# Router of 16 batches, fewer waits and another order on VectorE in a fused cross-attention and routed FFN

## The chip, the cores and the metric

The kernel runs on one core of one Trainium2 chip. The metric is the device time of one execution in microseconds (us), the median of several runs.

## The reference

`x` and the context are 128 batches of 128 tokens by 256 features, in float32. There is one layer, with 16 heads of 16 features:

```python
x = x + xattn(layernorm(x), ctx)      # q from x, k and v from ctx; softmax(q k / 4) v, then @ Wo + bo
n = layernorm(x)
scores = n @ w_router                 # per batch, 128 scores
top = top_k(scores, 96)               # of 128 tokens, in each batch
ffn = n, with rows `top` replaced by gelu(n[top] @ w_block)
x = x + ffn
```

The kernel finds the 32 tokens that are dropped, not the 96 that are kept: four rounds of "find the 8 largest of the negated scores, replace them".

## The kernel before

One batch is one tile of 128 x 256. All engines run the same software pipeline over s = 2 .. 127, each with its own order of calls written out by hand; semaphores alone tie them together. `upto(b)` is the count that a semaphore has once batch b is done. In pass s:

- TensorE: `scores(s)`, `transpose_inputs(s+5)` (normalised x and context), `values(s-1)`, queries or keys of a pair of batches (one of the two in each pass), `keep_columns`, `candidates` (each once in a group), `projection(s-2)`, `block_product(s-4)`, `transpose_x1(s-3)`, `attention(s-1)`. q, k and v are made in three matmuls of split float32 (hi and lo parts).
- ScalarE: `attention_copy(s-2)`, `gelu_tanh(s-7)`, `inputs_high(s+5)` (hi part of the transposed inputs), and 16 exponentials with their sums, in four blocks j = 3, 2, 1, 0 of four. `exp_ready[j]` signals each block.
- VectorE: `x1_transposed`, statistics, four `maxima(s, j)`, `inputs_low(s+5)` (lo part), `values_and_bias(s-1)` (makes v_sb), reciprocals, the biases of q or k, `residual(s-2)` (makes x1), `final(s-16)`, `stats2`, `product_scaled(s-4)` (makes z), and the router's steps.
- GpSimd: `normalise(s+7)`, reciprocal square roots, `values_over_sums(s-1)` (makes v_pad for attention), the polynomial and the products of gelu, x + bias, `unprocessed(s-16)` (the part of the result that the FFN leaves unprocessed).
- SyncE issues the loads of two batches at a time, eight copies that lay out each pair's queries (q_eo), and the stores of pairs.

PSUM has five banks for scores (bank J serves j = 0 in odd batches; the router's transposes share it), one for transposed inputs and z, one for attention, v and projection, one for q, k and transposed x1.

The router works on GROUP = 8 batches: `candidates(b)` transposes the scores of 8 batches to 8 partitions, `router(b, 0)` negates them, steps 1 to 8 are four times a maximum (MAX8) and a replacement (MATCH_REPLACE8), step 9 makes the row of kept tokens, `keep_columns(b)` transposes it back, step 10 makes `half_keep` and `drop_rstd`, and `scale_and_shift(b)` on GpSimd makes alpha and beta. `unprocessed` and `final` of the group follow. x1 and z are kept in rings of R = 16 batches. After pass 127 the end is written out by hand: it runs the last group's router once z(127) is there, then `unprocessed` of 8 batches (3 on GpSimd, 5 on ScalarE) and 8 finals on VectorE.

A wait is `engine.wait_ge(semaphore, count)`. In the program an instruction takes one of the waits in front of it along; the others become instructions of the sequencer.

Of the kernel before, what the change touches and what calls it, by code (L numbers as in the profile page):

```python
# [6 lines left out]
def cross_attention_routed_ffn(  # L7
# [33 lines left out]
    GROUP = 8  # L41
# [6 lines left out]
    with ctx:  # L48
# [41 lines left out]
        mv2 = sb("mv2", [P, R, 2])  # L90
        ve2 = sb("ve2", [P, R])
        rstd2 = sb("rstd2", [P, R])
# [104 lines left out]
        U_ON_ACT = tuple(range(B - 13, B - 8)) + tuple(range(B - 5, B))  # L197
# [6 lines left out]
        def _(sp):  # L204
# [16 lines left out]
            def store(b):  # L221

                if b % 2 == 0 and has(b):
                    sp.wait_ge(final_ready, upto(b + 1))
                    sp.dma_start(out[b:b + 2, :, :].rearrange("b t e -> t b e"),
                                 z_sb[:, b % R:b % R + 2, 0:E]).then_inc(stored[pair(b)], 16)
# [41 lines left out]
            for s in range(0, B + 18):  # L268
                queries_even_odd(s + 3)
                load_c(s + 8)  # L270
                store(s - 17)
# [5 lines left out]
        def _(pe):  # L277
# [24 lines left out]

            def scores(b):
# [4 lines left out]
                if h == 0:  # L308
                    pe.wait_ge(q_eo_in[r2], (b // 4 + 1) * 128)
                    pe.wait_ge(k_ready, upto(b + 1))  # L310
                if has(b - 1):
                    pe.wait_ge(exp_ready[3], upto(b - 1))
                    pe.wait_ge(exp_ready[1], upto(b - 1))
                    pe.wait_ge(exp_ready[2], upto(b - 1))
                if has(b - 2):
                    pe.wait_ge(exp_ready[0], upto(b - 2))
                if b % GROUP == 5 and has(b - 13):
                    pe.wait_ge(cand_ready, upto(b - 13 + 7))
                if b % GROUP == 1 and has(b - 17):
                    pe.wait_ge(keep_col_ready, upto(b - 17 + 7))  # L320
# [8 lines left out]
            def transpose_inputs(b):  # L329
# [3 lines left out]
                pe.wait_ge(xhat_ready, upto(b))  # L333
                if b % 2 == 0:
                    pe.wait_ge(c_in[pair(b)], landed(b))
# [14 lines left out]
            def transpose_x1(b):  # L350
# [3 lines left out]
                pe.wait_ge(x1_ready, upto(b))  # L354
# [6 lines left out]
                for c in range(C):  # L361
                    mm = nc.tensor.transpose(ps_xt[:, c * T:(c + 1) * T], x1_sb[:, b % R, c * P:(c + 1) * P], ident[:, :])
                mm.then_inc(xt_mm, 1)

            def attention(b):
# [3 lines left out]
                pe.wait_ge(v_pad_ready, upto(b))  # L369
# [29 lines left out]
            def block_product(b):  # L399
# [3 lines left out]
                pe.wait_ge(xt_ready, upto(b))  # L403
# [7 lines left out]
            def queries_or_keys(b, kind):  # L411
# [3 lines left out]
                w = "qk"[kind]  # L415
                if kind == 0:
                    pe.wait_ge(t_lo_ready, upto(b + 1))
# [4 lines left out]
                else:  # L422
                    pe.wait_ge(t_lo_ready, upto(b + 1))
# [12 lines left out]
            def projection(b):  # L436
# [3 lines left out]
                pe.wait_ge(o_ready, upto(b))  # L440
# [7 lines left out]
            def candidates(b):  # L448

                if b % GROUP == 0 and has(b):  # L450
                    pe.wait_ge(z_ready, upto(b + 7))
                    pe.wait_ge(exp_ready[0], upto(b + 11))
                    r = b % R
                    nc.tensor.transpose(ps_cand, z_sb[:, r:r + GROUP, E], ident[:, :]).then_inc(score_mm, 8)

            def keep_columns(b):

                if b % GROUP == 0 and has(b):
                    pe.wait_ge(keep_row_ready, upto(b + 7))
                    pe.wait_ge(exp_ready[0], upto(b + 15))  # L460
                    nc.tensor.transpose(ps_keep, keep_row[:, :], ident[0:GROUP, 0:GROUP]).then_inc(keep_mm, 8)
# [16 lines left out]
            queries_or_keys(4, 0)  # L478
            attention(0)

            for s in range(2, B - 1):
                scores(s)
                transpose_inputs(s + 5)
# [650 lines left out]
```

## Time and profile before

| | |
|---|---|
| median of 3 runs | 938.55 us (938.32 to 939.42) |
| the profiled execution | 938.16 us |
| its span, first to last instruction | 936.2 us |
| TensorE matmul, weight load busy | 896.5, 758.3 us |
| VectorE, ScalarE, GpSimd busy | 880.6, 875.5, 798.4 us |
| granted TensorE clock, mean | 0.988 |
| scores(12), scores(127) start at | 105.60, 901.92 us |

In the rows PE is TensorE's matmuls, PEld its weight loads, DVE VectorE, ACT ScalarE, POOL GpSimd, SPq SyncE's queue of DMA issues. L324 is line 324 of the kernel. A row of the timeline has start, duration, engine, line, operation, what it writes and reads, the number of merged instructions, and in brackets the engine's idle time before it and what ended it. The profile names x1_sb and x_sb alike as x_sb.

### The profile page before, as it was taken

To read this page: it belongs to the slowest core of one execution; us is meant where nothing else is said; L and a number is where in the kernel's file an instruction comes from. 1 tells how busy PE (TensorE), PEld (TensorE's weight loads), DVE (VectorE), ACT (ScalarE), POOL (GpSimd) and SP (SyncE) were. 2 spreads that over 40 slices of the span, in tenths; PEclk is the share of its full clock that TensorE was granted. 3 is DMA by queue.
4 is the path that set the end of the run, shared out by engine and by line. 5 is a ranking of instruction groups with operands and counts; after the bars stand their busy time and mean duration, and the time that the engine had idled before them with its cause. 6 is when DMAs were issued, how large, how long until landed. Compare 5 with 4: busy or idle time off the path is not lost. (4 is left out here: it accounts for less than half of the span.)

```text
span 936.2 us, 32893 instructions
## 1 busy us (share of the span) xinstructions
PE 896.5 (96%) x10296; PEld 758.3 (81%) x10296; DVE 880.6 (94%) x2318; ACT 875.5 (94%) x4499; POOL 798.4 (85%) x1488
## 2 busy tenths in 40 slices
PE   6899999999999999999999999999999999999972
PEld 5688888888888888888888888888888888888861
DVE  4898999999999999999999999999999999999877
ACT  2899999999999999999999999999999999999983
POOL 4367789999999999999999989999999999998865
PEclk8999999999999999999999999999999999999997
DMA  6222222232232232232223123223223223211102
GB/s 186 74 52 59 64 69 56 82 92 55 85 91 59 83 89 72 72 87 73 73 85 92 55 85 92 57 82 92 59 83 91 58 85 88 79 54 54 47 25 91
DMA packets 71244, 70.84 MB, mean 76 GB/s; under 512 B 12192, under 2 KB 62880, under 8 KB 71072
## 3 DMA queue, kind: packets, MB, share of 16 engines
q1 hardware_dynamic: 71072, 68.73, 25.6%
q8 instruction: 85, 1.39, 0.7%
q14 instruction: 87, 0.71, 0.2%
HBM read 35.13 MB, written 16.78 MB: 55 GB/s over the span
## 5 line engine op out<-in xcount | busy, mean ns | idle before, releaser
L532 ACT ACTIVATE e_sb<-ps_s,neg_max 128x128 f32<-128x128 f32 x2048 | 717.2, 411 | 8.3 <-DVE neg_max L644 8.2
L532 ACT ACTIVATION_READ_ACCUMULATOR e_sb<-ps_s,neg_max 128x1 f32 x2048 | 515.4, 252 | 0.0
L644 DVE TENSOR_REDUCE neg_max<-ps_s 128x4 f32<-128x512 f32 x512 | 330.5, 667 | 35.7 <-PE ps_s L324 35.2
L324 PE MATMUL ps_s<-q_eo,k_sb 32*128 32x256 f32 x2048 | 147.6, 401 | 9.7 <-DMA q_eo<-q_raw 3.6
L377 PE MATMUL ps_a<-e_sb,v_pad 128*32 128x128 f32 x4096 | 138.4, 276 | 2.1 <-POOL v_pad L969 0.7
L294 PE MATMUL ps_a<-w_o_sb,o_sb 128*128 128x256 f32 x512 | 135.7, 387 | 2.3 <-DVE v_sb L736 2.0
L969 POOL TENSOR_TENSOR v_pad<-v_sb,recip 128x256 f32<-128x256 f32 x128 | 79.4, 620 | 67.8 <-DVE recip L688 62.5
L294 PE MATMUL ps_t<-w_z_sb,xt_sb 128*128 128x258 f32 x512 | 132.7, 381 | 1.4 <-DVE z_sb L747 1.4
L324 PEld LDWEIGHTS ps_s<-q_eo,k_sb 32*128 32x128 f32 x2048 | 95.6, 185 | 39.0 <-issue 33.4
L377 PEld LDWEIGHTS ps_a<-e_sb,v_pad 128*32 128x32 f32 x4096 | 104.1, 109 | 24.0 <-issue 21.7
L959 POOL TENSOR_TENSOR x_sb<-x_sb,bo_sb 128x256 f32<-128x256 f32 x128 | 119.0, 931 | 0.2
L294 PEld LDWEIGHTS ps_t<-w_z_sb,xt_sb 128*128 128x128 f32 x512 | 97.3, 191 | 15.5 <-issue 2.0
L543 ACT CAST t_hi<-ps_t 128x512 fp32r<-128x512 f32 x127 | 74.5, 587 | 30.7 <-PE ps_t L347 28.4
L294 PEld LDWEIGHTS ps_a<-w_o_sb,o_sb 128*128 128x128 f32 x512 | 87.2, 189 | 13.8 <-issue 4.9
L1015 POOL TENSOR_TENSOR g_sb<-g_sb,z_sb 128x256 f32<-128x256 f32 x128 | 90.2, 705 | 0.3
L695 DVE TENSOR_TENSOR t_lo<-ps_t,t_hi 128x512 fp32r<-128x512 f32 x127 | 86.5, 681 | 0.9 <-ACT t_hi L543 0.8
L287 PE MATMUL ps_a<-w_v_hi,t_hi 128*128 128x256 f32 x256 | 83.4, 326 | 1.3 <-ACT o_sb L551 1.2
L1029 POOL TENSOR_TENSOR z_sb<-g_sb,z_sb 128x256 f32<-128x256 f32 x121 | 82.4, 681 | 0.0
L287 PE MATMUL ps_q<-t_hi,w_q_hi 128*128 128x256 f32 x256 | 73.0, 285 | 3.8 <-DVE t_lo L695 2.2
L998 POOL TENSOR_TENSOR g_sb<-z_sb 128x256 f32<-128x256 f32 x123 | 75.3, 612 | 0.3 <-DVE z_sb L747 0.3
L287 PE MATMUL ps_q<-t_hi,w_k_hi 128*128 128x256 f32 x256 | 72.7, 284 | 0.2 <-issue 0.2
L287 PE MATMUL ps_q<-t_hi,w_q_lo 128*128 128x256 f32 x256 | 72.7, 284 | 0.0
(92 smaller groups left out, 2199.2 us busy)
## 6 DMA issues: line engine op xcount, KB each, us to landing
x_sb<-in_x SPq DMA_DIRECT2D x64, 256.0 KB, 2.9
c_sb<-in_ctx SPq DMA_DIRECT2D x64, 256.0 KB, 3.1
q_eo<-q_raw SPq DMA_DIRECT2D x512, 32.0 KB, 2.0
out<-z_sb SPq DMA_DIRECT2D x64, 256.0 KB, 2.4
z_sb<-in_L_xattn_Wkv SPq DMA_DIRECT2D x2, 256.0 KB, 5.2
z_sb<-in_L_xattn_Wq SPq DMA_DIRECT2D x1, 256.0 KB, 3.1
w_z_sb<-in_L_ffn_w_block SPq DMA_DIRECT2D x1, 256.0 KB, 5.7
w_o_sb<-in_L_xattn_Wo SPq DMA_DIRECT2D x1, 256.0 KB, 3.0
```

Source lines behind the costliest of these rows:

```text
L287: last = nc.tensor.matmul(dst, lhs(a, c), rhs(b, c), start=(c == 0 and n == 0), stop=(c == C - 1 and n == len(terms) - 1))
L294: last = nc.tensor.matmul(dst, lhs(c), rhs(c), start=(c == 0), stop=(c == C - 1))
L324: mm = nc.tensor.matmul(ps_s[:, bank(b, j), c, :, :], k_sb[rows, r2, c, h * T:(h + 1) * T], q_eo[rows, r2, :, c, h, :], start=True, stop=True)
L377: mm = nc.tensor.matmul(ps_attn[32 * j:32 * j + 32, c * T:(c + 1) * T], v_pad[:, b % 2, c * J + j, par:par + 2, :].rearrange("p a d -> p ( ...
L532: last = nc.scalar.activation(e_sb[:, b % 4, j, c, par, :], ps_s[:, bank(b, j), c, par, :], ACT.Exp, bias=neg_max[:, b % 4, h:h + 1], accu ...
L644: nc.vector.tensor_reduce(neg_max[:, b % 4, :].rearrange("p (c j q) -> p j c q", c=C, j=J)[:, j, :, :], ps_s[:, bank(b, j), :, :, :], AX.X ...
L695: nc.vector.tensor_tensor(t_lo[part].rearrange("p k c t -> p (k c) t"), inputs_bank(b)[:, :].rearrange("p (n t) -> p n t", t=T), t_hi[part ...
L959: nc.gpsimd.tensor_tensor(x_sb[:, b % R, :], x_sb[:, b % R, :], bo_sb[:, :], ALU.add).then_inc(xb_ready, 1)
L969: nc.gpsimd.tensor_tensor(v_pad[:, b % 2, :, 0:3:2, :], v_sb[:, b % 2, :].rearrange("p (g q d) -> p g q d", q=2, d=D), recip[:, b % 4, :]. ...
L998: nc.gpsimd.tensor_tensor(g_sb[:, b % 4, :], z_sb[:, b % R, 0:E], z_sb[:, b % R, 0:E], ALU.mult).then_inc(square_ready, 1)
L1015: nc.gpsimd.tensor_tensor(g_sb[:, b % 4, :], g_sb[:, b % 4, :], z_sb[:, b % R, 0:E], ALU.mult).then_inc(cubic_ready, 1)
L1029: nc.gpsimd.tensor_tensor(z_sb[:, b % R, 0:E], g_sb[:, b % 4, :], z_sb[:, b % R, 0:E], ALU.mult).then_inc(gelu_ready, 1)
```

## The change

- GROUP is 16 and not 8. x1, z and their statistics are kept in rings of Q = 32 batches. `final`, `unprocessed` and the stores come 24 batches behind instead of 16 (stores 25 instead of 17).
- The router's steps stand in other passes: one replacement near a pass's start and one maximum near its end, over four passes, with step 9 ahead of `values_and_bias`.
- `values_and_bias` stands ahead of `inputs_low` on VectorE.
- TensorE: `scores` waits for `exp_ready[1]` alone. The waits for the pair's q_eo and k, for the inputs (xhat, context), for the scaled values and for the router's bank are calls of their own, earlier in the pass.
- Each engine's functions have a parameter `settled`. In passes 32 to about 126 (`sure`) it leaves out waits that another wait implies.
- In the end's hand-written order the last group has 16 batches: 16 finals behind its router, `unprocessed` of 6 on GpSimd and 10 on ScalarE.

```diff
-    GROUP = 8
+    GROUP = 16
+    Q = 32
     R = 16
-        x1_sb = sb("x1_sb", [P, R, E])
+        x1_sb = sb("x1_sb", [P, Q, E])
-        z_sb = sb("z_sb", [P, R, ZW])
+        z_sb = sb("z_sb", [P, Q, ZW])
-        U_ON_ACT = tuple(range(B - 13, B - 8)) + tuple(range(B - 5, B))
+        U_ON_ACT = tuple(range(B - 21, B - 16)) + tuple(range(B - 10, B))
...
+            def pair_ready(b, settled=False):
+                if b % 2 == 0 and has(b):
+                    pe.wait_ge(q_eo_in[(b // 2) % 2], (b // 4 + 1) * 128)
+                    if not settled:
+                        pe.wait_ge(k_ready, upto(b + 1))
+            def inputs_ready(b):
+                if has(b):
+                    pe.wait_ge(xhat_ready, upto(b))
+                    if b % 2 == 0:
+                        pe.wait_ge(c_in[pair(b)], landed(b))
             def scores(b):
...
-                if h == 0:
-                    pe.wait_ge(q_eo_in[r2], (b // 4 + 1) * 128)
-                    pe.wait_ge(k_ready, upto(b + 1))
+                if b == 0:
+                    pair_ready(b)
                 if has(b - 1):
-                    pe.wait_ge(exp_ready[3], upto(b - 1))
                     pe.wait_ge(exp_ready[1], upto(b - 1))
-                    pe.wait_ge(exp_ready[2], upto(b - 1))
-                if has(b - 2):
-                    pe.wait_ge(exp_ready[0], upto(b - 2))
-                if b % GROUP == 5 and has(b - 13):
-                    pe.wait_ge(cand_ready, upto(b - 13 + 7))
-                if b % GROUP == 1 and has(b - 17):
-                    pe.wait_ge(keep_col_ready, upto(b - 17 + 7))
+            def router_bank_free(b):
+                if b % GROUP == 5 and has(b - 21):
+                    pe.wait_ge(cand_ready, upto(b - 21 + 15))
+                if b % GROUP == 9 and has(b - 25):
+                    pe.wait_ge(keep_col_ready, upto(b - 25 + 15))
...
             for s in range(2, B - 1):
+                sure = 32 <= s < B - 8
                 scores(s)
-                transpose_inputs(s + 5)
+                transpose_inputs(s + 5, s > 2)
                 values(s - 1)
-                queries_or_keys(s + 2, 1)
-                queries_or_keys(s + 3, 0)
-                keep_columns(s - 16)
-                candidates(s - 12)
-                projection(s - 2)
-                block_product(s - 4)
-                transpose_x1(s - 3)
-                attention(s - 1)
+                queries_or_keys(s + 2, 1, sure)
+                queries_or_keys(s + 3, 0, sure)
+                keep_columns(s - 24)
+                candidates(s - 20)
+                projection(s - 2, sure)
+                pair_ready(s + 1, sure)
+                inputs_ready(s + 6)
+                block_product(s - 4, sure)
+                if sure:
+                    scaled_values_ready(s - 1)
+                transpose_x1(s - 3, sure)
+                router_bank_free(s + 1)
+                attention(s - 1, sure)
...
             for s in range(2, B):
-                x1_transposed(s - 4)
+                sure = 32 <= s < B - 1
+                x1_transposed(s - 4, sure)
                 if s >= 4:
                     stats1(s + 10)
                 aggregate2(s - 3)
-                router(s - 15, 6)
+                router(s - 21, 2)
+                router(s - 22, 4)
+                router(s - 23, 6)
+                router(s - 24, 8)
                 if s >= 4:
                     aggregate1(s + 10)
                 maxima(s, 3)
                 maxima(s, 2)
+                router(s - 24, 9)
+                values_and_bias(s - 1, sure)
                 inputs_low(s + 5)
-                values_and_bias(s - 1)
                 inverse_sums(s - 1)
                 maxima(s, 1)
-                queries(s + 3)
-                router(s - 16, 10)
-                router(s - 14, 5)
-                router(s - 15, 7)
-                router(s - 13, 2)
-                router(s - 12, 0)
-                keys(s + 2)
-                residual(s - 2)
+                queries(s + 3, sure)
+                router(s - 24, 10)
+                router(s - 20, 0)
+                keys(s + 2, sure)
+                residual(s - 2, sure)
                 maxima(s, 0)
...
-                router(s - 12, 1)
-                router(s - 13, 3)
-                final(s - 16)
+                router(s - 20, 1)
+                router(s - 21, 3)
+                router(s - 22, 5)
+                router(s - 23, 7)
+                final(s - 24, sure)
                 stats2(s - 2)
-                router(s - 15, 8)
-                product_scaled(s - 4)
-                router(s - 13, 4)
-                router(s - 15, 9)
+                product_scaled(s - 4, sure)
...
-            final(B - 11)
-            for step in range(9):
-                router(B - 8, step)
-            router(B - 8, 9)
+            for step in range(10):
+                router(B - 16, step)
+            final(B - 18)
+            router(B - 16, 10)
+            final(B - 17)
             gelu_product(B - 3)
-            router(B - 8, 10)
             gelu_product(B - 2)
             gelu_product(B - 1)
-            final(B - 10)
-            final(B - 9)
-            for b in range(B - 8, B):
+            for b in range(B - 16, B):
                 final(b)
```

## Rows read from the trace of the kernel before

**Rows 1.** The page, part 1: busy time, share of the span, instructions.

```profile
PE 896.5 (96%) x10296; PEld 758.3 (81%) x10296; DVE 880.6 (94%) x2318; ACT 875.5 (94%) x4499; POOL 798.4 (85%) x1488
```

**Rows 2.** Waits: who waited for what, us in total, times, longest.

```profile
PEld ps_t L347 <- issue: 37.8, 113, 0.7
DVE neg_max L644 <- PE ps_s L324: 35.2, 72, 4.3
PEld ps_s L324 <- issue: 33.4, 127, 2.3
ACT t_hi L543 <- PE ps_t L347: 28.4, 93, 4.4
```

**Rows 3.** Timeline of weight loads: scores(12), scores(118), scores(119).

```profile
105.60 0.77 PEld L324 LDWEIGHTS ps_s<-q_eo,k_sb 32*128 32x128 f32 x16 [0.29 <-issue]
...
840.97 0.74 PEld L324 LDWEIGHTS ps_s<-q_eo,k_sb 32*128 32x128 f32 x16 [0.20 <-issue]
...
847.75 0.31 PEld L324 LDWEIGHTS ps_s<-q_eo,k_sb 32*128 32x128 f32 x8 [0.20 <-issue]
```

**Rows 4.** Timeline of weight loads: scores(66) to scores(69), and projection in step 67.

```profile
480.31 0.77 PEld L324 LDWEIGHTS ps_s<-q_eo,k_sb 32*128 32x128 f32 x16 [0.29 <-issue]
...
487.12 0.74 PEld L324 LDWEIGHTS ps_s<-q_eo,k_sb 32*128 32x128 f32 x16 [0.20 <-issue]
...
490.75 0.73 PEld L294 LDWEIGHTS ps_a<-w_o_sb,o_sb 128*128 128x128 f32 x4
...
494.01 0.77 PEld L324 LDWEIGHTS ps_s<-q_eo,k_sb 32*128 32x128 f32 x16 [0.29 <-issue]
...
500.92 0.74 PEld L324 LDWEIGHTS ps_s<-q_eo,k_sb 32*128 32x128 f32 x16 [0.20 <-issue]
```

**Rows 5.** Timeline of ScalarE: end of block 1, start of block 3, end of block 1.

```profile
486.62 0.28 ACT L532 ACTIVATION_READ_ACCUMULATOR e_sb<-ps_s,neg_max 128x1 f32 x1
...
489.38 0.37 ACT L532 ACTIVATE e_sb<-ps_s,neg_max 128x128 f32<-128x128 f32 x1
...
493.40 0.28 ACT L532 ACTIVATION_READ_ACCUMULATOR e_sb<-ps_s,neg_max 128x1 f32 x1
```

**Rows 6.** Timeline of VectorE: steps 67 and 68 from their first maxima, then steps 69 and 70.

```profile
488.42 1.29 DVE L644 TENSOR_REDUCE neg_max<-ps_s 128x4 f32<-128x512 f32 x2 [0.27 <-PE ps_s L324]
...
490.22 0.41 DVE L736 TENSOR_TENSOR v_sb<-ps_a,bv_sb 128x256 f32<-128x256 f32 x1
...
495.30 0.69 DVE L644 TENSOR_REDUCE neg_max<-ps_s 128x4 f32<-128x512 f32 x1 [0.36 <-PE ps_s L324]
...
502.40 1.26 DVE L644 TENSOR_REDUCE neg_max<-ps_s 128x4 f32<-128x512 f32 x2
...
509.43 0.66 DVE L644 TENSOR_REDUCE neg_max<-ps_s 128x4 f32<-128x512 f32 x1
```

**Rows 7.** Timeline of GpSimd: v_pad in steps 67 and 68.

```profile
490.87 0.62 POOL L969 TENSOR_TENSOR v_pad<-v_sb,recip 128x256 f32<-128x256 f32 x1 [0.40 <-DVE recip L688]
...
497.76 0.62 POOL L969 TENSOR_TENSOR v_pad<-v_sb,recip 128x256 f32<-128x256 f32 x1 [0.34 <-DVE recip L688]
```

**Rows 8.** Groups by line, the router's maxima and replacements: busy us, mean ns | idle.

```profile
L773 DVE MAX8 top<-cand 8x8 f32<-8x128 f32 x64 | 17.3, 271 | 0.4
L767 DVE MATCH_REPLACE8 cand<-top,cand 8x128 f32<-8x128 f32 x64 | 16.9, 264 | 0.0
```

**Rows 9.** Timeline of weight loads: projection in step 68, behind the candidates' transpose.

```profile
497.75 0.73 PEld L294 LDWEIGHTS ps_a<-w_o_sb,o_sb 128*128 128x128 f32 x4
```

**Rows 10.** The end: timeline of GpSimd and of VectorE.

```profile
928.11 2.47 POOL L1046 TENSOR_SCALAR x_sb<-x_sb,alpha,beta 128x256 f32<-128x256 f32 x3
...
930.61 2.46 DVE L798 SCALAR_TENSOR_TENSOR z_sb<-z_sb,half_keep,x_sb 128x256 f32<-128x256 f32 x6 [0.30 <-POOL x_sb L1046]
```

**Rows 11.** The window from 932 to 934 us: busy by engine, clock, DMA share, GB/s.

```profile
932.00:934.00 2.00, 0.00 (x0) 0.00 (x0) 1.07 (x3) 0.00 (x0) 0.00 (x0) 0.50 0.78 259
```

**Rows 12.** GpSimd's x + bias, line 959: duration ns min/median/max, first and last start.

```profile
L959 POOL TENSOR_TENSOR x_sb<-x_sb,bo_sb x128: 722/957/1317, 14.1 to 880.7; 128x256 f32<-128x256 f32 x128
```

More of the change, by code:

```diff
@@ L266, in _ @@
             queries_even_odd(2)
-            for s in range(0, B + 18):
+            for s in range(0, B + 26):
                 queries_even_odd(s + 3)
                 load_c(s + 8)
-                store(s - 17)
+                store(s - 25)
                 load_x(s + 13)
@@ L526, in exps @@
                 act.wait_ge(max_ready[j], upto(b))
-                if j == 3 and has(b - 4):
+                if j == 3 and has(b - 4) and not settled:
                     act.wait_ge(a_mm, upto(b - 4))
@@ L535, in exps, with inputs_high @@
                 last.then_inc(exp_ready[j], 1)
-            def inputs_high(b):
+            def inputs_high(b, settled=False):
                 if has(b):
                     act.wait_ge(t_mm, upto(b))
-                    if has(b - 8):
+                    if has(b - 8) and not settled:
                         act.wait_ge(v_mm, upto(b - 8))
@@ L544, in inputs_high, with attention_copy @@
                                    inputs_bank(b)[:, :].rearrange("p (n t) -> p n t", t=T)).then_inc(t_hi_ready, 1)
-            def attention_copy(b):
+            def attention_copy(b, settled=False):
                 if has(b):
                     act.wait_ge(a_mm, upto(b))
-                    if has(b - 2):
+                    if has(b - 2) and not settled:
                         act.wait_ge(o_mm, upto(b - 2))
@@ L609, in _ @@
             gelu_tanh(B - 6)
-            for b in range(B - 13, B - 8):
+            for b in range(B - 21, B - 16):
                 unprocessed(b)
@@ L619, in _ @@
             gelu_tanh(B - 1)
-            for b in range(B - 5, B):
+            for b in range(B - 10, B):
                 unprocessed(b)
@@ L698, in inputs_low, with queries @@
                                             ALU.subtract).then_inc(t_lo_ready, 1)
-            def queries(b):
+            def queries(b, settled=False):
                 if b % 2 == 0 and has(b):
                     dve.wait_ge(q_mm, upto(b + 1))
-                    if has(b - 4):
+                    if has(b - 4) and not settled:
                         dve.wait_ge(q_eo_in[(b // 2) % 2], b // 4 * 128)
@@ L713, in queries, with keys @@
                                             ALU.add).then_inc(q_raw_ready, 2)
-            def keys(b):
+            def keys(b, settled=False):
                 if b % 2 == 0 and has(b):
                     dve.wait_ge(k_mm, upto(b + 1))
-                    if has(b - 4):
+                    if has(b - 4) and not settled:
                         dve.wait_ge(s_mm[J - 1], upto(b - 3))
@@ L883, in _ @@
             inverse_sums(B - 1)
-            router(B - 16, 10)
+            final(B - 24)
             x1_transposed(B - 3)
@@ L890, in _ @@
             aggregate2(B - 2)
-            final(B - 16)
-            final(B - 15)
+            final(B - 23)
+            final(B - 22)
             x1_transposed(B - 2)
@@ L947, in normalise @@
                     pool.wait_ge(rstd1_ready, upto(b))
-                    if has(b - 4):
+                    if has(b - 4) and not settled:
                         pool.wait_ge(t_mm, upto(b - 4))
@@ L1098, in _ @@
             gelu_cubic(B - 4)
-            unprocessed(B - 14)
+            unprocessed(B - 22)
             rstd2_of_one(B - 1)
@@ L1106, in _ @@
             gelu_cubic(B - 1)
-            scale_and_shift(B - 8)
-            for b in range(B - 8, B - 5):
+            scale_and_shift(B - 16)
+            for b in range(B - 16, B - 10):
                 unprocessed(b)
```

204 lines of the change are left out of this document (108 added, 96 removed).

## The prediction

> **What bounds the kernel now.** I read the page first, then the waits, then TensorE's weight loads over whole steps (its matmuls' ends are modelled, the starts of its loads are not), then the other engines against the same steps, and last the end.
>
> The page shows four engines between 85% and 96% busy, so busy time alone names none of them [rows 1]. In the waits VectorE waits 35.2 us in all for scores and ScalarE 28.4 us for transposed inputs. TensorE's own idle time has the label "issue": 37.8 us before the transposes and 33.4 before the scores [rows 2]. So the others wait for TensorE, and TensorE waits for nothing that is named.
>
> A step s is one pass of the main loop; I measure it from the first load of scores(s) to that of scores(s + 1). scores(12) starts at 105.60 and scores(118) at 840.97: 735.37 us for 106 steps, 6.94 each [rows 3]. Steps 66, 67 and 68 start at 480.31, 487.12 and 494.01 and step 69 at 500.92: 6.81, 6.89 and 6.91 us [rows 4]. Step 118 takes 6.78 [rows 3]. The gap before the transposes is 0.33 each time (37.8 us in 113 times) [rows 2]; that before the scores is 0.20 in steps 67 and 69 and 0.29 in steps 66 and 68 [rows 4]. Both stand where TensorE's tiles change shape. Scores of an odd b have four waits, those of 69 (b % 8 is 5) five, and both show 0.20; scores of an even b have six. So the gap is 0.20 whatever the waits, up to a point that the even steps pass.
>
> Why the even ones pass it: ScalarE finishes the third block of exponentials (exp_ready[1]) at 486.62 + 0.28 = 486.90, 0.22 before scores(67), and at 493.40 + 0.28 = 493.68, 0.33 before scores(68) [rows 5]. Behind that signal the odd step needs at most 0.22 and the even one, with two waits more, 0.33.
>
> VectorE has 0.36 us idle in a plain cycle of 6.88 us (488.42 to 495.30, first maximum to first maximum) and none in step 69's, 502.40 to 509.43, 7.03 us: that one holds router work [rows 6]. In step 67 v_sb ends at 490.22 + 0.41 = 490.63 and the projection, which waits for it, starts at 490.75, 3.63 into the step [rows 4, 6]: there is no room, and whatever makes VectorE late makes the projection late. So plain steps are TensorE's, and most router steps are VectorE's.
>
> **The change, part by part.**
>
> *Waits ahead of the scores.* Only exp_ready[1] stays; the pair's waits go ahead of the block product of the step before. Odd steps keep their 0.20. Even steps lose 0.09 (0.29 to 0.20), so that each step becomes one like step 118, 6.78 us. Left is what signal to start costs with one wait. It is not in the trace; it lies between nothing and 0.22. In the new step the signal comes at about 6.57 (486.90 - 480.31 = 6.59; 493.68 - 487.12 = 6.56). With nothing the scores are bound by TensorE, at 6.78. With 0.22 they start at 6.79 to 6.81, 0.02 more. I take 0, since 0.22 holds three more waits.
>
> *Other waits left out on TensorE.* They stand inside runs of long matmuls or in front of the 0.33 gap, which is the same for the inputs of odd b, with two waits, and of even b, with three. I cost them at nothing. The waits put earlier (pair, inputs, scaled values) must be done by then, for the block product, x1's transposes and attention are queued behind them. GpSimd issues `normalise(s + 6)` in its pass s - 1, and TensorE asks for it in step s. v_pad is ready at 490.87 + 0.62 = 491.49 [rows 7]; its wait now stands behind projection (490.75, 0.73 long) and block product. The copies of q_eo are issued two steps ahead. They cost nothing.
>
> The Trainium skill (Advanced Engine Details and Errata, Network/Comms) gives 50 to 100 ns for a sequencer's reading of a semaphore. Our 0.09 for two waits agrees; the equal gaps of 0.20 and 0.33 say that the rest is hidden. By the rule for every wait the sum would be another one (rival 5).
>
> *Waits left out on ScalarE, VectorE and GpSimd.* VectorE's work in step 69 stands without idle time, whatever waits lie between (no row of it has a gap) [rows 6]. Cost nothing, gain nothing.
>
> *values_and_bias ahead of inputs_low.* It moves inputs_low (0.68, of which 0.07 overlaps what follows) from in front of v_sb to behind it. v_sb then ends 2.9 into the step instead of 3.51; the projection falls back to TensorE's own order. In plain steps that gives about 0.01 (6.78 to 6.77); its worth is in router steps, where VectorE may now be up to 0.6 late. inputs_low ends at 3.6 instead of 3.2; its first reader is the block product, at 4.38 (projection plus 0.75), so 0.8 covers it.
>
> *Router of 16.* Maximum and replacement run along 128 elements in 8 partitions, and now in 16; I take the same time. 16 groups of 11 instructions become 8: half of 17.3 and 16.9 us for the maxima and replacements and of smaller ones, over 17 us of VectorE's time less [rows 8]. TensorE has 0.11 for the candidates' transpose (projection at 497.75 - 494.01 = 3.74 against 3.63) [rows 4, 9]; the keep column's is a transpose too, and I give it the same and 0.04 for its wait, together 0.26, now once in 16 steps.
>
> *Steps spread.* Five steps in 16 hold about 0.46 us of router (a maximum of 0.27 and a replacement of 0.26, each overlapping the next by 0.07 [rows 8], and the loading of values, 0.07). VectorE's plain work is 6.88 - 0.36, less some 0.1 of small waits, 6.42. A router step is then 6.88 against 6.77: it falls back by 0.1 a step, 0.5 in five. It comes about 0.3 early to the first maximum, and ScalarE starts exponentials at 489.38 [rows 5], 0.3 after the first maximum is ready (488.42 + 0.69): 0.6 covers 0.5. I take 0.1 for each 16 steps.
>
> *The step.* 6.77 + (0.26 + 0.1) / 16 = 6.79.
>
> *The end.* The last group is 16 batches: 16 instead of 8 finals stand behind the last router. Now three `unprocessed` on GpSimd take 928.11 to 930.58, 0.79 apart, and the last six finals 930.61 to 933.07, 0.396 apart [rows 10]. With six on GpSimd the sixth ends at 928.11 + 6 x 0.79 = 932.85. ScalarE's ten run beside them; even at 0.5 each they end by 933.1, ahead of their finals. Ten more finals: the last starts at 932.9 + 10 x 0.396 = 936.86 and ends at 937.35, 4.3 later. The bounds: 0.56 for a GpSimd operation without VectorE beside it gives 2.9; stores are the other end: five pairs in 4 us are 328 GB/s, where 259 is what the rows show [rows 11], so up to 1.1 more. I take 4.6. The eight finals and `unprocessed` of the group before stand where eight stood before, in idle time.
>
> **The sum.** Steps 12 to 117: 106 x (6.937 - 6.79) = 15.6. Steps 2 to 11, without router: 10 x (6.85 - 6.77) = 0.8. Steps 118 to 126: 0.8 for the five that still run in full and for the even ones behind them. Together 17.2, less 4.6: 12.6. The profiled execution took 938.16 us (span 936.2 and 2.0 around it), 0.4 below the median: 938.55 - 12.6 = 926.0.
>
> **Rivals.**
>
> 1. *VectorE still sets the router steps* (13%). If they stay 0.26 over 6.77, as step 69 is, each group of 16 has 1.3 instead of 0.1: 6.6 groups, 7.9 less gain, 934; with half of it absorbed by the room that values_and_bias gives, 930, the likelier. For: 6.42 + 0.46 is over 6.77, and GpSimd's work beside them can lengthen finals. Against: the room of 0.6.
>
> 2. *GpSimd becomes the bound, and the kernel slower* (6%). A plain cycle of it is 490.87 to 497.76 less 0.34 idle, 6.55 [rows 7]. x + bias took between 0.72 and 1.32 us, median 0.96 [rows 12], by what VectorE ran beside it. The Trainium skill (Advanced Engine Details and Errata, GPSIMD Details) says that Pool and VectorE share an interface when VectorE has two inputs in SBUF; that range agrees. With a maximum put ahead of each final the overlaps shift. It decides from a GpSimd cycle of 6.90 (6.94 - 4.6/122): 0.35 more in every step, which is the whole of 1.32 - 0.96. At 1.32 and 0.1 more in its neighbours the step is 7.0: 122 x 0.06 + 4.6 = 12 slower, 950. Against: only router steps shift.
>
> 3. *No gain in plain steps* (5%): the even steps wait 0.29 for something else. Only router excess is halved, about 4.9; the end takes 4.6: 938, no change.
>
> 4. *The odd gap is waits too* (6%): 0.045 a wait, three fewer: 6.64, where ScalarE's signal at 6.57 lets it. 122 x 0.13 = 16 more: 910. Against: 0.20 for four waits and for five.
>
> 5. *The skill's rule for every wait* (2%): some seven waits fewer on TensorE in 88 steps at 50 to 100 ns would be 31 to 62 us: 865 to 895. The rows' equivalent, seven at 0.045, is 28 us, 898.
>
> **How the numbers follow.** My forecast has 68%: 926, with a range of its own of 922.5 to 929.5 (the end from 2.9 to 5.7 and 0.02 to 0.03 a step for the signal). With rival 1, most of which lies below 932, that is about 80%: 922 to 932. A measurement of this kernel can tell about 0.2%, 1.9 us. Faster: 68 + 13 + 6 + 2 = 89%; same 5%; slower 6%.
>
> **What would show it.** Scores' loads 6.77 apart in odd and even steps, both with a gap of 0.20; the projection 3.60 to 3.63 into nearly every step; VectorE's idle time before the first maximum about 0.25 in plain steps and near none in five of 16; the gap of 0.33 as before; the last final about 4.4 us further behind the last router than now. It is wrong if even steps keep 0.29, if GpSimd loses its idle time before v_pad, or if the odd gap shrinks.

## The result and the profile after

The changed kernel takes 933.94 us (median of 4 runs, 932.71 to 934.11), the kernel before 938.84 beside it (4 runs, 938.32 to 939.42): ratio 0.9944, 95% interval 0.9930 to 0.9958. It is faster by 4.9 us, 0.5%, and the interval leaves out 1; 12.6 were forecast, and 933.9 lies outside the range of 922 to 932. The profiled execution took 934.11, span 932.0.

The page after, part 1 (compare [rows 1]), and its waits (compare [rows 2]; us in total, times, longest):

```profile
PE 890.2 (96%) x10280; PEld 755.5 (81%) x10280; DVE 860.3 (92%) x2190; ACT 878.1 (94%) x4504; POOL 787.0 (84%) x1467
```

```profile
POOL v_pad L1000 <- DVE recip L716: 65.3, 112, 3.9
DVE neg_max L671 <- PE ps_s L330: 45.3, 104, 5.0
PEld ps_t L359 <- issue: 39.4, 117, 0.7
PEld ps_a L395 <- issue: 25.5, 126, 4.0
...
PEld ps_s L330 <- ACT e_sb L558: 23.3, 105, 2.3
```

VectorE has 20 us less work and waits 10 us more for scores; the gap before the transposes is still 0.34 (39.4 in 117 times). The name on the gap before the scores is new, since only one wait is left there, but its size is the old 0.20 of the odd steps. One row is a warning: a single wait of 4.0 us in front of attention.

TensorE's weight loads in the changed kernel, scores and projections of steps 66, 67, 70 and 72, and scores(118):

```profile
475.22 0.74 PEld L330 LDWEIGHTS ps_s<-q_eo,k_sb 32*128 32x128 f32 x16 [0.20 <-ACT e_sb L558]
478.83 0.74 PEld L295 LDWEIGHTS ps_a<-w_o_sb,o_sb 128*128 128x128 f32 x4
482.01 0.74 PEld L330 LDWEIGHTS ps_s<-q_eo,k_sb 32*128 32x128 f32 x16 [0.20 <-ACT e_sb L558]
...
502.48 0.74 PEld L330 LDWEIGHTS ps_s<-q_eo,k_sb 32*128 32x128 f32 x16 [0.20 <-ACT e_sb L558]
506.20 0.74 PEld L295 LDWEIGHTS ps_a<-w_o_sb,o_sb 128*128 128x128 f32 x4
509.38 0.74 PEld L330 LDWEIGHTS ps_s<-q_eo,k_sb 32*128 32x128 f32 x16 [0.20 <-issue]
...
516.16 0.74 PEld L330 LDWEIGHTS ps_s<-q_eo,k_sb 32*128 32x128 f32 x16 [0.20 <-ACT e_sb L558]
519.98 0.13 PEld L481 LDWEIGHTS ps_s<-ident,keep_row 16*128 16x128 f32 x1
520.14 0.73 PEld L295 LDWEIGHTS ps_a<-w_o_sb,o_sb 128*128 128x128 f32 x4
523.30 0.74 PEld L330 LDWEIGHTS ps_s<-q_eo,k_sb 32*128 32x128 f32 x16 [0.20 <-issue]
...
829.90 0.74 PEld L330 LDWEIGHTS ps_s<-q_eo,k_sb 32*128 32x128 f32 x16 [0.20 <-ACT e_sb L558]
```

Even steps now show 0.20 as odd ones do (0.29 in [rows 4]), and a plain step is 6.79 (475.22 to 482.01; eleven plain steps, 73 to 83, take 74.67 us, 6.788 each). In every 16 steps three are longer: 6.89 with the candidates, 6.90 in step 70, and 7.14 in step 72, which holds the keep column (516.16 to 523.30). There the projection starts 3.98 into the step instead of 3.61.

The prediction left open what it costs to get from ScalarE's signal to the scores' load, between nothing and 0.22. Step 70 answers it. The exponentials that scores(70) waits for end here:

```profile
502.09 0.27 ACT L558 ACTIVATION_READ_ACCUMULATOR e_sb<-ps_s,neg_max 128x1 f32 x1
```

That ends at 502.36, 0.12 before the load at 502.48; in front of scores(67), in a plain stretch, it is 0.24 (481.49 + 0.28 = 481.77, and 482.01). The later signal changes nothing: the gap is 0.20 all the same and step 69 takes 6.79. So the way from signal to load takes at most 0.12, and a plain step is set by TensorE itself.

All runs are compared by the same cuts, made at the first loads of scores(2), scores(118) and scores(127). Stretches are us of one profiled execution of each kernel; "behind" is from scores(2) to the end of the span. Medians hold the start too, and the start differs from run to run (last section). From 2 to 118 the kernels with the same loop (changed, e1, e3 and e7) agree within 0.1 us. The stretches:

| kernel | median | start to 2 | 2 to 118 | 118 to 127 | 127 to end | behind |
|---|---|---|---|---|---|---|
| before | 938.84 | 37.26 | 803.71 | 60.95 | 34.28 | 898.94 |
| changed | 933.94 | 39.41 | 790.49 | 60.48 | 41.64 | 892.61 |
| e1, finals later | 929.61 | 37.68 | 790.50 | 60.47 | 38.98 | 889.95 |
| e2, keep column over 128 rows | 931.68 | 37.57 | 789.86 | 60.33 | 41.97 | 892.16 |
| e3, the left-out waits put back | 932.73 | 39.29 | 790.58 | 60.47 | 41.64 | 892.69 |
| e4, before + waits moved | 933.31 | 37.63 | 798.41 | 60.45 | 34.81 | 893.67 |
| e5, e4 + values ahead | 929.45 | 36.98 | 794.73 | 60.43 | 34.26 | 889.42 |
| e6, changed, values back | 933.94 | 38.17 | 791.80 | 60.34 | 41.89 | 894.03 |
| e7, rows in turn | 931.79 | 37.90 | 790.50 | 60.47 | 40.15 | 891.12 |
| e8, e1 + e2 + e7 | 927.53 | 37.13 | 789.88 | 60.33 | 37.99 | 888.20 |
| e9, one exponentials' wait | 932.93 | 37.20 | 798.43 | 60.49 | 34.79 | 893.71 |
| e10, pair's waits moved | 934.39 | 37.84 | 798.67 | 60.52 | 34.73 | 893.92 |
| e11, e5 mended alike | 929.56 | 39.52 | 794.58 | 60.37 | 34.05 | 889.00 |

From before to changed: the start gives 2.15 more, the steps 13.69 less (13.22 and 0.47), the end 7.36 more: 4.18 less in the span. The forecast was 0, 17.2 less and 4.6 more.

The extra in the end stands in VectorE's timeline, right behind the loop:

```profile
898.56 0.21 DVE L716 RECIPROCAL recip<-sums 128x16 f32<-128x16 f32 x1
902.17 0.78 DVE L829 SCALAR_TENSOR_TENSOR z_sb<-z_sb,half_keep,x_sb 128x256 f32<-128x256 f32 x1 [3.39 <-POOL x_sb L1078]
902.87 0.41 DVE L680 COPY xt_sb<-ps_q 128x256 f32<-128x256 f32 x1
...
904.93 0.47 DVE L829 SCALAR_TENSOR_TENSOR z_sb<-z_sb,half_keep,x_sb 128x256 f32<-128x256 f32 x1
907.95 0.48 DVE L829 SCALAR_TENSOR_TENSOR z_sb<-z_sb,half_keep,x_sb 128x256 f32<-128x256 f32 x1 [2.55 <-POOL x_sb L1078]
```

and in the loads of the last attention:

```profile
904.45 1.51 PEld L395 LDWEIGHTS ps_a<-e_sb,v_pad 128*32 128x32 f32 x32 [4.02 <-issue]
```

`final(B - 24)` now stands in front of x1's copy, the scaled product and the residual. It waits 3.39 us for its `unprocessed` row, which GpSimd has only at 902.1, behind v_pad and the cubic. Queued behind it is `residual(B - 2)`, and attention(B - 1) waits for that, 4.02 us where the kernel before shows 1.11. `final(B - 22)` stops VectorE again, for 2.55.

### The profile page after: what moved, and what is told of

Same layout as the page of the kernel before. It is cut to its first block, busy times and chain, and to the rows that moved or that the text cites. A ratio compares the mean times of both kernels' runs of the same rounds, so it can differ in the third digit from the quotient of the medians.

```text
span 932.0 us, 30875 instructions
## 1 busy us (share of the span) xinstructions
PE 890.2 (96%) x10280; PEld 755.5 (81%) x10280; DVE 860.3 (92%) x2190; ACT 878.1 (94%) x4504; POOL 787.0 (84%) x1467
## 4 chain that ended last, share of the span: by engine, by line
PE 91%; ACT 3%; DVE 2%; issue 1%; POOL 1%; DMA 1%; SPq 1%; POOLq 0%; DVEq 0%
PE ps_q L288 19%; PE ps_s L330 15%; PE ps_a L395 13%; PE ps_a L295 12%; PE ps_t L295 11%; PE ps_a L288 10%; PE ps_t L359 8%; PE ps_q L375 3%; ACT e_sb L558 2%; DMA x_sb<-in_x 1%; DVE z_sb L829 0%; POOL x_sb L1078 0%; SPq L241 0%; DVE neg_max L671 0%; POOL g_sb L1046 0%
## 5 line engine op out<-in xcount | busy, mean ns | idle before, releaser
L295 PE MATMUL ps_a<-w_o_sb,o_sb 128*128 128x256 f32 x512 | 133.1, 382 | 1.8 <-DVE v_sb L764 1.8
L330 PEld LDWEIGHTS ps_s<-q_eo,k_sb 32*128 32x128 f32 x2048 | 93.4, 186 | 35.3 <-ACT e_sb L558 23.3
L989 POOL TENSOR_TENSOR x_sb<-x_sb,bo_sb 128x256 f32<-128x256 f32 x128 | 114.4, 895 | 0.2
L288 PE MATMUL ps_q<-t_lo,w_q_hi 128*128 128x256 f32 x256 | 73.5, 287 | 0.0
```

What stands on the lines that cost most here:

```text
L288: last = nc.tensor.matmul(dst, lhs(a, c), rhs(b, c), start=(c == 0 and n == 0), stop=(c == C - 1 and n == len(terms) - 1))
L295: last = nc.tensor.matmul(dst, lhs(c), rhs(c), start=(c == 0), stop=(c == C - 1))
L330: mm = nc.tensor.matmul(ps_s[:, bank(b, j), c, :, :], k_sb[rows, r2, c, h * T:(h + 1) * T], q_eo[rows, r2, :, c, h, :], start=True, stop=True)
L989: nc.gpsimd.tensor_tensor(x_sb[:, b % R, :], x_sb[:, b % R, :], bo_sb[:, :], ALU.add).then_inc(xb_ready, 1)
```

## The experiments

Eleven kernels, each timed beside the kernel before on the same chip. Ratios are to that, with 95% intervals.

**e1: are the finals queued too early?** In VectorE's end:

```
-            final(B - 24)
             x1_transposed(B - 3)
...
-            final(B - 23)
-            final(B - 22)
             x1_transposed(B - 2)
...
             x1_transposed(B - 1)
-            final(B - 21)
+            final(B - 24)
+            final(B - 23)
+            final(B - 22)
             gelu_product(B - 5)
             product_scaled(B - 2)
+            final(B - 21)
             final(B - 20)
```

> The changed kernel, with the finals of batches B-24 to B-20 moved later on VectorE behind the loop, to behind x1_transposed(B-1), the rest untouched. Theory 1 (finals queued too early): in the changed kernel VectorE stands still 3.39 us and 2.55 us in front of final(B-24) and final(B-22), and TensorE's attention of batch B-1 waits 4.02 us where it waited 1.1 before; the end behind the scores of batch 127 falls from 41.6 to 38.5 to 39 us, the time from 933.9 to about 931. Theory 2 (the end is set by the sixteen finals behind the last router alone, and VectorE's idle time is cover): no change, 933.9. Theory 3 (the finals moved back only pile up in front of the last router): as late as before or up to 1 us later, 934 to 935.

929.61 us, ratio 0.9900 (0.9885 to 0.9915). The end fell from 41.64 to 38.98, 2.66 less, and each stretch of the steps stayed the same to 0.01, as theory 1 has it. The other 1.7 of the gain in the medians lies ahead of scores(2). In e1's loads and finals:

```profile
900.01 0.84 PEld L395 LDWEIGHTS ps_a<-e_sb,v_pad 128*32 128x32 f32 x32 [1.29 <-POOL v_pad L1000]
```

```profile
904.51 1.41 DVE L829 SCALAR_TENSOR_TENSOR z_sb<-z_sb,half_keep,x_sb 128x256 f32<-128x256 f32 x3
```

The last attention waits 1.29, not 4.02, and the finals run with no gap in front of them.

**e2: what is the keep column's price?** keep_row is cleared once, ahead of the loop; the router writes its first 16 rows.

```
-        keep_row = sb("keep_row", [GROUP, T])
+        keep_row = sb("keep_row", [P, T])
...
-                    nc.tensor.transpose(ps_keep, keep_row[:, :], ident[0:GROUP, 0:GROUP]).then_inc(keep_mm, 16)
+                    nc.tensor.matmul(ps_keep, keep_row[:, :], ident[:, 0:GROUP], start=True, stop=True).then_inc(keep_mm, 16)
```

> The changed kernel, with the row of kept tokens held in 128 partitions, 112 of them zero, and turned by a matmul over all 128 rows and 16 columns instead of a transpose over 16 rows. The step with the keep column takes 7.14 us where the plain one takes 6.79. Theory 1 (the price is that the weight load of 16 rows can't begin behind the key matmuls as one of 128 rows can: the load stands 0.33 us behind the load before it): 0.2 to 0.25 less in each of seven steps, 1.5 to 1.8 us in all, 932.2, and the step takes 6.90 to 6.95. Theory 2 (VectorE is late in this step, and the projection waits for it): no change, 933.9 and 7.14.

931.68 us, ratio 0.9917 (0.9903 to 0.9931); behind scores(2) 0.45 less: the steps 0.78 less, the end 0.33 more, for which no cause was looked for. The other 1.8 of the 2.3 us between the medians lies ahead of scores(2). Step 72 in e2:

```profile
513.98 0.74 PEld L330 LDWEIGHTS ps_s<-q_eo,k_sb 32*128 32x128 f32 x16 [0.20 <-ACT e_sb L558]
517.59 0.31 PEld L481 LDWEIGHTS ps_s<-ident,keep_row 128*128 128x128 f32 x2
517.82 0.73 PEld L295 LDWEIGHTS ps_a<-w_o_sb,o_sb 128*128 128x128 f32 x4
520.99 0.74 PEld L330 LDWEIGHTS ps_s<-q_eo,k_sb 32*128 32x128 f32 x16 [0.20 <-issue]
```

The load now starts 3.61 into the step, where the projection's would, instead of 3.82 (519.98 - 516.16), and the step takes 7.01. That is 0.13 less, where 0.20 to 0.25 was expected. So theory 1 holds for part of the price: the late start of the load is gone. What remains, 0.22 over a plain step, is the 0.23 by which the projection's load stands behind this tile's (517.82 - 517.59); the candidates' transpose costs 0.10. Why this one costs more was not tried. The edit makes a plain matmul of the transpose too; the rows and the operation were not tried apart.

**e3: do waits that hold already cost anything?** Every `sure = 32 <= s < ...`, in the loops of TensorE, ScalarE, VectorE and GpSimd, became `sure = False`.

> The changed kernel with every wait that it leaves out between steps 32 and 119 put back (on all four engines); the order of the work and the places of the other waits are as changed. Theory 1 (a wait whose condition holds already costs nothing that the period shows, as the prediction took it): 933.9 within 1 us, plain steps at 6.79. Theory 2 (each such wait costs its engine time, and TensorE's count): 5 to 7 waits on TensorE a step; already 0.01 us each would be 5 us over 88 steps, 939; the Trainium skill gives more for one (Advanced Engine Details and Errata, Network/Comms).

932.73 us, ratio 0.9931 (0.9919 to 0.9944), and 892.69 behind scores(2) where the changed kernel has 892.61. Steps are the same to a hundredth. So theory 1 holds, and rival 5 falls. The Trainium skill (Advanced Engine Details and Errata, Network/Comms) gives 50 to 100 ns for a sequencer's reading of a semaphore; in the traces TensorE waits for 15 or 16 semaphores in each of steps 66 and 67 of e3 and for 11 in the changed kernel, so by that page the 4 or 5 more would be, as an estimate, some 20 us over 88 steps. The traces don't agree: the waits put back cost nothing that shows.

**e4: the waits in front of the scores alone**, in the kernel before:

```
             def scores(b):
-                if h == 0:
-                    pe.wait_ge(q_eo_in[r2], (b // 4 + 1) * 128)
-                    pe.wait_ge(k_ready, upto(b + 1))
+                if b == 0:
+                    pair_ready(b)
                 if has(b - 1):
-                    pe.wait_ge(exp_ready[3], upto(b - 1))
                     pe.wait_ge(exp_ready[1], upto(b - 1))
-                    pe.wait_ge(exp_ready[2], upto(b - 1))
...
                 projection(s - 2)
+                pair_ready(s + 1)
                 block_product(s - 4)
                 transpose_x1(s - 3)
+                router_bank_free(s + 1)
                 attention(s - 1)
```

> The kernel before, with one part of the change alone: in front of the scores stands only the wait for exp_ready[1]; the waits for queries and keys stand behind the projection, those for the router's bank in front of the attention. Groups stay at 8. Theory 1 (the even steps' gap of 0.29 us in front of the scores was 0.20 and the waits): 0.09 less in each of 61 even steps, 5.5 us in all, 933.3. Theory 2 (the gap closed in the changed kernel because VectorE's order changed): no change, 938.8. Together with the changed kernel's time it also says what the groups of 16 bring in all: the loop lost 12.5 us, so some 7 of them would be the router's, and the end gave 7.4 back.

933.31 us, ratio 0.9932 (0.9919 to 0.9944): this one part gives as much as the whole change (0.9944, and the intervals overlap). Behind scores(2) it is 5.27 less, all of it between scores(2) and scores(118): 58 even steps of 0.09 are 5.2. Every plain step is 6.79 there too. Steps 69 and 70 of e4:

```profile
498.08 0.74 PEld L328 LDWEIGHTS ps_s<-q_eo,k_sb 32*128 32x128 f32 x16 [0.20 <-issue]
501.88 0.73 PEld L294 LDWEIGHTS ps_a<-w_o_sb,o_sb 128*128 128x128 f32 x4
505.04 0.74 PEld L328 LDWEIGHTS ps_s<-q_eo,k_sb 32*128 32x128 f32 x16 [0.20 <-issue]
508.91 0.73 PEld L294 LDWEIGHTS ps_a<-w_o_sb,o_sb 128*128 128x128 f32 x4 [0.20 <-issue]
512.07 0.74 PEld L328 LDWEIGHTS ps_s<-q_eo,k_sb 32*128 32x128 f32 x16 [0.20 <-issue]
```

```profile
508.38 0.41 DVE L743 TENSOR_TENSOR v_sb<-ps_a,bv_sb 128x256 f32<-128x256 f32 x1
```

These take 6.96 and 7.03. In step 70 the projection waits for v_sb, which ends at 508.79; it follows at 508.91, 3.87 into the step.

**e5: e4 and the values' bias ahead**, groups still of 8:

```
-                inputs_low(s + 5)
                 values_and_bias(s - 1)
+                inputs_low(s + 5)
```

> The kernel before with two parts of the change: the waits in front of the scores as in e4, and VectorE's values_and_bias in front of inputs_low. Groups stay at 8. The run with the waits alone has, in every eight steps, 0.35 (keep column), 0.09 (candidates), 0.17 and 0.24 us over the plain 6.79; in the last two the projection waits for v_sb, done at 3.68 and 3.75 us of the step. Theory 1 (VectorE is late in these two steps and the values' bias, now ahead, takes their excess away): 0.17 and most of 0.24 less in each eight steps, 5 us in all against 933.3, so 928 to 929; the group of 16 then brings nothing: it takes some 3 us of router steps away in the loop and gives more than that back at the end. Theory 2 (the lateness is VectorE's whole work, and another instruction is late in place of v_sb): 933.3, and the group of 16 with its spread steps is what shortens the loop.

929.45 us, ratio 0.9896 (0.9881 to 0.9911): 4.5 us faster than the changed kernel, which differs from it by the groups of 16, the spread steps and the waits left out. Theory 1 holds in the main. Steps 69 and 70 take 6.79 and 6.91, and step 71 6.86 (0.07 passed on); 4.25 less than e4 behind scores(2). From here to the changed kernel the steps lose 4.19 and the end gains 7.38, so groups of 16 with their spread steps cost 3.19 us as built.

**e6: the values' bias back, in the changed kernel.**

> The changed kernel with VectorE's values_and_bias back behind inputs_low. Theory 1 (the prediction's: in plain steps the projection's load has room enough, 0 there; it matters only in the steps where VectorE is late): plain steps at 6.79, steps 6 and 8 of 16 a little longer, by 0.05 to 0.3 us together, 0.3 to 2 us in all. Theory 2 (in plain steps too the projection would wait for v_sb): each step 0.05 to 0.1 longer, 5 to 11 us in all. Theory 3: nothing at all.

933.94 us, ratio 0.9943 (0.9931 to 0.9956); 1.42 more behind scores(2), 1.17 of them in the steps. Plain steps stay 6.79. Step 69 becomes 7.08, since the projection waits:

```profile
498.87 0.73 PEld L295 LDWEIGHTS ps_a<-w_o_sb,o_sb 128*128 128x128 f32 x4 [0.23 <-DVE v_sb L764]
```

while step 70 falls to 6.79. Theory 1 holds: the same edit is worth 4.25 with groups of 8 and 1.42 with groups of 16. Half as many steps hold router work there, and the steps stand in other passes; the two were not tried apart.

**e7: the last unprocessed rows in turn.** The lists change, and the last loops of ScalarE and GpSimd with them.

```
+        LAST_ON_POOL = tuple(range(B - 15, B - 3, 2))
-        U_ON_ACT = tuple(range(B - 21, B - 16)) + tuple(range(B - 10, B))
+        U_ON_ACT = tuple(b for b in range(B - 21, B) if b not in LAST_ON_POOL)
```

> The changed kernel with one edit in its end: of the last sixteen batches GpSimd makes the unprocessed rows of B-15, B-13, ... B-5 in place of the first six, and ScalarE the ten others in place of the last ten. Theory 1 (behind the last router the finals go at GpSimd's pace, 0.784 us for one of six, while ScalarE's are ready early; with both feeding in turn VectorE goes at its own 0.396): the sixteen finals take 6.4 us instead of 8.4, 2.0 to 2.3 us less in all. Theory 2 (the stores set the end, DMA at 0.99 of its share from 928 on): the finals end 2 us earlier and the last store less than 1 us earlier.

931.79 us, ratio 0.9918 (0.9904 to 0.9931); the end is 1.49 shorter, not 2.0 to 2.3. The last finals of the changed kernel and then of e7:

```profile
924.12 0.48 DVE L829 SCALAR_TENSOR_TENSOR z_sb<-z_sb,half_keep,x_sb 128x256 f32<-128x256 f32 x1 [0.30 <-POOL x_sb L1078]
924.90 4.45 DVE L829 SCALAR_TENSOR_TENSOR z_sb<-z_sb,half_keep,x_sb 128x256 f32<-128x256 f32 x11 [0.30 <-POOL x_sb L1078]
```

```profile
919.16 7.21 DVE L831 SCALAR_TENSOR_TENSOR z_sb<-z_sb,half_keep,x_sb 128x256 f32<-128x256 f32 x16
```

The gaps of 0.30 are gone, but sixteen finals take 7.21 us, 0.45 each, where eleven in a row took 4.45, 0.40 each. The span ends 2.7 us behind the last final in both kernels, so the stores follow the finals and don't set the end (theory 2 falls).

**e8: e1, e2 and e7 together.**

> The changed kernel with the three edits together: finals B-24 to B-20 later in the end, the keep column from 128 rows, the last unprocessed rows in turn from ScalarE and GpSimd. If they add: behind scores(2) 2.7 and 0.8 and 2.2 less, 5.7 in all against 892.6 there, so 886.9; the whole 927 to 928.5 by how the start falls out (it takes up to 2 us more in some runs than in others). If the finals overlap with what the later ones wait for: 0.5 to 1 us less gain.

927.53 us, ratio 0.9874 (0.9861 to 0.9888), the fastest: 11.9 us ahead of the kernel before on that chip (939.40) and 6.4 of the changed one. Behind scores(2) 4.41 less than the changed kernel, where the three alone add to 4.60 (5.7 had been expected from the sizes hoped for).

**e9 and e10: why 0.29 in even steps?** e9 leaves the pair's two waits in front of the scores, drops three of the exponentials' and moves the router bank's; e10 moves the pair's two and keeps all the others.

> The kernel before; in front of the scores only one wait for the exponentials is left (exp_ready[1]), the router's bank is waited for in front of the attention, and the two waits for the pair (q_eo_in, k_ready) stay in front of the even scores. In the trace of before the even scores' waits are three semaphore instructions 0.107 us apart and a fourth that the load carries, the first ended at -0.24 us by exp_ready[1]; in odd steps one instruction ends at -0.185 and the load follows at 0. Theory 1 (nothing is late; the count of wait instructions that stand behind the one for exp_ready[1] sets the gap): with three waits the even gap is 0.20, all steps plain at 6.79, 933.3. Theory 2 (the pair's own waits are what is late, queries or keys arriving just then): the even gap stays 0.29, 938.8. Theory 3: half of it.

> The kernel before; only the two waits for the pair (q_eo_in, k_ready) move from the front of the even scores to behind the projection; the four waits for exponentials stay, and those for the router's bank. Theory 1 (count of wait instructions behind exp_ready[1]'s): even steps become as odd ones, gap 0.20, period 6.79, 933.3. Theory 2 (four waits for exponentials are themselves too many): the even gap stays over 0.20 in part, 935 to 937.

932.93 (ratio 0.9931, 0.9916 to 0.9946) and 934.39 (0.9948, 0.9932 to 0.9965). Scores of 66 and 67 in e9, then in e10:

```profile
477.16 0.74 PEld L323 LDWEIGHTS ps_s<-q_eo,k_sb 32*128 32x128 f32 x16 [0.20 <-issue]
483.94 0.74 PEld L323 LDWEIGHTS ps_s<-q_eo,k_sb 32*128 32x128 f32 x16 [0.20 <-ACT e_sb L532]
```

```profile
477.97 0.74 PEld L329 LDWEIGHTS ps_s<-q_eo,k_sb 32*128 32x128 f32 x16 [0.20 <-issue]
484.75 0.74 PEld L329 LDWEIGHTS ps_s<-q_eo,k_sb 32*128 32x128 f32 x16 [0.20 <-issue]
```

Either edit gives the whole gain: 893.71 and 893.92 behind scores(2), against 893.67 in e4. The pair's waits stay in front in e9 and the exponentials' in e10, and both kernels have the gap of 0.20, so no single wait was late. The semaphore records of the traces show that it was their number: in even steps of the kernel before three semaphore instructions stand some 0.107 apart behind the last attention load, the first done at -0.24 with exp_ready[1], and the scores' load at 0. In odd steps only one stands there, done at -0.185; in the even steps of e9 it is one too, done at -0.144, and of e10 one, done at -0.182. With one, the load keeps TensorE's own gap of 0.20; with three it comes 0.09 later.

**e11: groups of 8, mended alike** (e5 with e2's keep column and e7's turns for the last eight).

> The kernel before with the two parts that paid (waits in front of the scores as in e4, values_and_bias ahead), groups still of 8, and with the keep column turned over 128 rows as in e2 and the last eight unprocessed rows in turn from ScalarE and GpSimd as in e7. Against e5 (889.4 us behind scores(2)): the keep column 0.11 to 0.13 less in each of 14 steps, 1.6 to 1.9; the end 0.5 to 0.8 less. So 886.9 to 887.4 behind scores(2), 1 us ahead of e8 with its groups of 16 (888.2), and 926 to 928.5 in all by the start. If groups of 16 are worth having once their end is mended: 889 or more.

929.56 us, ratio 0.9895 (0.9880 to 0.9910); 889.00 behind scores(2), so the expectation of 886.9 to 887.4 fell. Step 72 is 7.00 instead of 7.12, but step 73 is 6.84 instead of 6.77: 0.07 of the 0.12 comes back, and other steps give the rest, for the steps as a whole lose 0.15. With groups of 8 VectorE has no idle time left around these steps; with groups of 16 the same edit kept its 0.13. So the groups of 16 are worth 0.8 us, once their end is mended (888.20), and cost 3.2 without. The 0.8 rests on one profile of each; the ratios' intervals (0.9861 to 0.9888 for e8, 0.9880 to 0.9910 here) touch.

## Why the prediction was wrong

The direction was right and so was the mechanism of the loop. Three terms of the sum were off, the end's first of all, and the start, which is in no term, differed in the profiled run. In the span 8.4 us are missing (12.6 - 4.18), in the medians 7.7; in this order:

- *"The eight finals and `unprocessed` of the group before stand where eight stood before, in idle time"*: this step failed, and 2.66 us with it (e1). I counted VectorE's idle time and not its order. What stands in `router(B - 16, 10)`'s place is a wait for GpSimd, ahead of the residual on which TensorE's last attention depends, and GpSimd in turn waits for VectorE's sums of that residual. The rest of the term held: from the last half_keep to the last final it was 5.8 us and is 10.2, the 4.4 more that the prediction gave as a sign.
- *The plain step*: 6.788, not 6.77. Step 118 of the kernel before was rounded down to 6.78 (its loads are 6.788 apart in the trace's own ns), and the gain of 0.01 from values_and_bias wasn't there (e6: plain steps the same). 0.018 in the 116 steps from 2 to 118 is 2.1 us.
- *The keep column, "I give it the same and 0.04 for its wait"*: 0.35, not 0.15, in 7 steps: 1.4 us. I priced a transpose over 16 rows by one over 128. The load's late start is part of the difference (e2); the rest I can't split. The trace of the kernel before had the price, in a step that I didn't look at, its step 72:

```profile
521.82 0.77 PEld L324 LDWEIGHTS ps_s<-q_eo,k_sb 32*128 32x128 f32 x16 [0.33 <-issue]
...
528.96 0.74 PEld L324 LDWEIGHTS ps_s<-q_eo,k_sb 32*128 32x128 f32 x16 [0.20 <-issue]
```

That is 7.14, where the even step 66 took 6.81: 0.33 for the keep column.

- *The start*: 2.15 us later at scores(2), discussed below; its cause stays open. Without it the time would be about 931.8, just inside the range, and that would have been luck, with the end and the loop 6.3 us off.

Right were: the even steps' 0.09 (e4, 5.3 us), against rival 3; 0.20 in odd steps whatever the waits, against rival 4; the waits left out at nothing (e3); v_sb's end at 2.92 (477.72 + 0.42 - 475.22) and VectorE's idle 0.26 in plain steps; the "0.1 for each 16 steps" for VectorE's lateness (step 70 takes 0.11 more). Rival 1 thus fell; without values_and_bias ahead 1.4 of its 7.9 us would have come (e6). GpSimd never became the bound in the loop (rival 2); in the end VectorE did wait for it. The prediction's "agrees" for 0.09 over two waits was too kind: that is 0.045 for each, below the range that it was held against. My account of the values' bias understated it: its worth was in router steps, as said, but it was 4.25 us at groups of 8, as much as the groups of 16 bring to the loop afterwards.

## What to carry to other kernels

When a group grows, look at the drain code that is written out by hand: whatever a longer pipeline moves into an old slot must be checked for what it waits on and who is queued behind it, not for idle time alone. Count the wait instructions that stand behind the one that is signalled last: here those ahead of it were free, and three of them, 0.107 us apart, were too many for a gap of 0.20. When a step of one kind is priced, look for it in the trace before pricing it by another. Try the parts of a change alone and cut every run at the same points; here one cheap part gave as much as the whole, two gave 9.5 (898.94 - 889.42), and the costly third had to be mended before it paid.

## What the runs showed of the hardware

**The start differs from run to run by up to 2.5 us.** scores(2) came between 36.98 and 39.52 in the profiled runs. e1, e2, e3, e7 and the changed kernel have the same start but for e2's clearing and e3's waits, and range from 37.57 to 39.41. The windows 20 to 35 us, of the changed kernel and of e1 (us, then busy of PE, PEld, DVE, ACT, POOL, granted clock, DMA share, GB/s):

```profile
20.00:25.00 5.00, 3.82 (x25) 3.02 (x26) 1.59 (x3) 0.86 (x5) 0.00 (x0) 0.55 0.79 249
25.00:30.00 5.00, 3.46 (x17) 2.99 (x16) 4.18 (x10) 4.03 (x20) 1.06 (x3) 0.77 0.13 37
30.00:35.00 5.00, 4.46 (x31) 3.71 (x32) 2.83 (x6) 3.52 (x21) 2.45 (x4) 0.66 0.35 89
```

```profile
20.00:25.00 5.00, 3.92 (x27) 3.13 (x28) 1.69 (x3) 0.96 (x6) 0.00 (x0) 0.66 0.80 235
25.00:30.00 5.00, 2.75 (x24) 2.07 (x26) 4.33 (x11) 4.86 (x25) 1.33 (x4) 1.00 0.15 45
30.00:35.00 5.00, 3.48 (x38) 2.94 (x30) 4.01 (x8) 4.32 (x24) 2.20 (x4) 1.00 0.28 70
```

In the first TensorE has the lower of its two levels (1.2 GHz) for part of all three windows, and 17 matmuls take 3.46 us; in the second it has 2.4 GHz (granted 1.00) from 25 us on. Mean clocks over the whole run go with it: e1 took 929.4 to 929.7 at 0.988 and 931.18 at 0.981. Why the clock rises sooner in one run than in the next stays open. e11, with groups of 8, had the late start too (0.53, 0.79 and 0.66 in these windows), so it needs no group of 16. But the runs of the kernels with groups of 16 have mean clocks of 0.979 to 0.989 and the others 0.983 to 0.992, so whether the change makes a late start more frequent is not shown either way. Of the 1.2 us between the medians of the changed kernel and of e3 the start is the likely cause, which is argued and not shown.

**GpSimd's `unprocessed` row took 0.55 us early in the end and 0.79 behind the last router** (1.09 us for two at 901.58, 4.76 for six at 920.10), where finals on VectorE and rows on ScalarE run beside it. In e7, where the finals run without a gap, it took 0.92 (5.53 us for six), and the finals stretched from 0.40 to 0.45. Which of the other engines stretches it was not tried. The rows of the changed kernel, then e7's:

```profile
901.58 1.09 POOL L1078 TENSOR_SCALAR x_sb<-x_sb,alpha,beta 128x256 f32<-128x256 f32 x2
...
920.10 4.76 POOL L1078 TENSOR_SCALAR x_sb<-x_sb,alpha,beta 128x256 f32<-128x256 f32 x6
```

```profile
918.59 5.53 POOL L1080 TENSOR_SCALAR x_sb<-x_sb,alpha,beta 128x256 f32<-128x256 f32 x6
```
